# Turned-row copies, query statistics, late rows and first expert rows in another order (attention, router and experts on one core)

## The reference, cut to what matters

```python
# x (4, 1024, 256), ctx (4, 154, 256); 16 heads of 16; 8 experts of width 192, top 2; one shared expert
q = layernorm_heads(layernorm(x) @ Wq.T) * SCALE     # in heads of 16
k = layernorm_heads(ctx @ Wk.T); v = ctx @ Wv.T
x = x + (softmax(q @ k.T) @ v) @ Wp.T + bp
h = layernorm(x)
scores = sigmoid(h @ W_gate_router)
sel = top_k(scores + expert_bias, 2); w = scores[sel] / sum(scores[sel])
shared = (silu(h @ Wg_s) * (h @ Wu_s)) @ Wd_s
routed = sum over the two e in sel of w_e * (silu(h @ Wg[e]) * (h @ Wu[e])) @ Wd[e]
return x + shared + routed
```

## Time and profile before

| | |
|---|---|
| median of three runs | 539.19 us |
| profiled execution, its own time | 539.25 us |
| its span | 537.4 us |
| mean granted TensorE clock | 0.971 |
| PE, DVE, ACT, POOL busy | 476.9, 314.9, 300.8, 213.2 us |
| attention loop | to about 253 us |
| shared stage | to about 332 us |
| experts | from 337 us |

### The profile page before, as it was taken

The page is one execution under the profiler, slowest core; times in us unless marked ns, Lnnn a source line. Parts: engine busy times, 40 slices in busy tenths (PEclk is TensorE's granted clock), DMA queues, the critical chain, the costliest instruction groups (busy, mean ns, idle before and its releaser), DMA issues.

```text
span 537.4 us, 12057 instructions
## 1 busy us (share of the span) xinstructions
PE 476.9 (89%) x3324; PEld 313.0 (58%) x3325; DVE 314.9 (59%) x965; ACT 300.8 (56%) x544; POOL 213.2 (40%) x186
## 2 busy tenths in 40 slices
PE   4867899999899979888999995799999998999990
PEld 3743344444444435333554542799989987988980
DVE  3995466767877587555837872255555545445550
ACT  1577878888777785565333011455655654555540
POOL 4113211111011853045453253056655557555654
PEclk9999999999999998899999999699999999999996
DMA  7959301111101311033347554545766756575654
GB/s 232 339 187 355 155 20 40 41 41 56 39 26 39 121 67 54 20 119 127 119 139 233 162 189 138 148 79 98 122 97 94 125 85 100 99 118 88 102 79 46
DMA packets 43703, 60.99 MB, mean 113 GB/s; under 512 B 6512, under 2 KB 34672, under 8 KB 42992
## 3 DMA queue, kind: packets, MB, share of 16 engines
q1 hardware_dynamic: 28768, 37.45, 23.0%
q0 software_dynamic: 14896, 23.08, 21.5%
HBM read 34.29 MB, written 29.39 MB: 118 GB/s over the span
## 4 chain that ended last, share of the span: by engine, by line
PE 47%; DVE 12%; issue 11%; DMA 11%; ACT 11%; POOL 2%; SPq 2%; POOLq 2%; DVEq 0%; ACTq 0%
PE bankS L1114 7%; PE bankS L1105 7%; ACT attn L642 6%; DMA out<-VR,attn 6%; PE bankV L939 5%; PE bankR L795 4%; PE bankS L1033 4%; PE bankQ L1105 3%; PE bankR L1105 3%; DMA sorted_rows<-XR,route 3%; PE bankV L943 2%; POOL sorted_rows L496 2%; PE bankQ L795 2%; DVE OTT L1337 1%; DVE rec L1335 1%
## 5 line engine op out<-in xcount | busy, mean ns | idle before, releaser
L553 POOL DMA_INDIRECT out<-VR,attn x71 | 109.6, 1544 | 91.1 <-DVE VR L1573 40.7
L496 POOL DMA_INDIRECT sorted_rows<-XR,route x64 | 63.5, 993 | 86.3 <-PE bankD L945 22.8
L642 ACT ACTIVATE attn<-bankS,bias 128x512 f32<-128x512 f32 x128 | 81.0, 680 | 11.9 <-PE bankS L911 11.6
L755 ACT ACTIVATE attn<-experts 128x768 f32 x72 | 60.5, 843 | 24.0 <-issue 23.9
L939 PE MATMUL bankV<-attn,VS 128*32 128x512 f32 x256 | 62.8, 613 | 3.7 <-DVE OTT L1337 3.5
L941 PE MATMUL bankD<-attn,ON 128*32 128x512 f32 x256 | 62.8, 613 | 0.0
L1105 PE MATMUL bankS<-scores_in,attn 128*128 128x128 f32 x432 | 55.2, 287 | 2.8 <-issue 2.6
L1105 PEld LDWEIGHTS bankS<-scores_in,attn 128*128 128x128 f32 x432 | 52.1, 199 | 9.0 <-issue 9.0
L472 POOL DMA_DIRECT2D x_in<-in_xT x13 | 9.5, 735 | 113.0 <-PE bankQ L795 112.0
L1573 DVE TENSOR_TENSOR VR<-bankS,attn 128x256 f32<-128x256 f32 x71 | 30.2, 425 | 27.3 <-PE bankS L1114 14.0
L1114 PE MATMUL bankS<-experts,scores_in 128*128 x142 | 42.7, 383 | 0.4 <-DVE VR L1573 0.3
(11 more groups left out here) (272 smaller groups left out, 951.9 us busy)
## 6 DMA issues: line engine op xcount, KB each, us to landing
VS<-sorted_rows SPq DMA_DIRECT2D x72, 130.0 KB
x_cols<-X2T SPq DMA_DIRECT2D x16, 256.0 KB
out<-X SPq DMA_DIRECT2D x8, 512.0 KB
x_in<-in_xT POOLq DMA_DIRECT2D x15, 256.0 KB, 3.6
scores_in<-x_cols SPq DMA_DIRECT2D x14, 256.0 KB
experts<-in_wgu SPq DMA_DIRECT2D x2, 1536.0 KB, 9.7
X<-in_x SPq DMA_DIRECT2D x1, 2048.0 KB, 18.4
experts<-in_wd SPq DMA_DIRECT2D x2, 1024.0 KB, 14.8
```

What stands on the lines that cost most here:

```text
L496: pool.indirect_dma_start(sorted_rows.rearrange("s p r -> (s p) r"), bass.IndirectOffsetOnAxis(ap=index, axis=0), rows, None, bounds_check ...
L553: pool.indirect_dma_start(out, bass.IndirectOffsetOnAxis(ap=dest[:, i:i + 1], axis=0), y_out[:, i % 4], None, bounds_check=B * N + SPARE - ...
L642: act.activation(Pb[:, u % 2, c, :], bankS[:, c % GH, :], ACT.Exp, bias=bias[:, b, GH * g + c:GH * g + c + 1] if c < GH else biasR[:, b, g ...
L755: act.activation(w_cur[:, k], wgu_sb[:, :, ds(e_, 1), :].rearrange("p c o f -> p c (o f)"), ACT.Copy).then_inc(f_w["e"], 1)
```

## The change

- ScalarE, even units from 26 on: `out_columns(m)` stands ahead of `denominators(u - 2)` and the fifth exponential, not behind them.
- VectorE, units 16 and 24 (where the first selection of a part, `scored` and `best(0)`, stands in the odd unit just before): `stats` stands behind `norm`, ahead of `spreads`.
- Shared stage, TensorE: the late rows are turned ahead of the first two parts of step 2; the logits go ahead of `shared_down(1)`; `counts` of the last part go from step 4 to step 3, there behind `shared_down(2)`. ScalarE: the exponential of the last logits stands between the two gates of step 2. VectorE: the last part's selection, sums and places move ahead of shared products.
- Experts: the second half of the first group's rows is turned behind `up(1)` and copied behind the first gate.

```diff
--- before.py
+++ after.py
@@ -688,10 +688,12 @@
                         if m >= 0:
                             out_root(m)
                         exps(u, (2, 3))
+                        if pc >= PIECES:
+                            out_columns(m)
                         if u >= 2:
                             denominators(u - 2)
                         exps(u, (4,))
-                        if m >= 0:
+                        if m >= 0 and pc < PIECES:
                             out_columns(m)
                         c, step = divmod(m, PP)
                         if c >= 1 and step == 0:
@@ -741,13 +743,10 @@
                 act.activation(late_r[:, k], late_mv[:, k, :, 1], ACT.Ln, bias=eps[:, :]).then_inc(l_ln, 1)
                 act.wait_ge(l_ln, k + 1)
                 act.activation(late_r[:, k], late_r[:, k], ACT.Exp, scale=-0.5).then_inc(l_or, 1)
-            def columns(a):
-
-
-                for h in range(2):
-                    act.wait_ge(f_xt["e"], 2 * a + (h + 1))
-                    act.activation(x_col[:, 2 * h:2 * h + 2], row_bank(h).rearrange("p (t c) -> p t c", t=2), ACT.Copy) \
-                        .then_inc(f_xc["e"], 1)
+            def columns(a, h):
+
+                act.wait_ge(f_xt["e"], 2 * a + (h + 1))
+                act.activation(x_col[:, 2 * h:2 * h + 2], row_bank(h).rearrange("p (t c) -> p t c", t=2), ACT.Copy).then_inc(f_xc["e"], 1)
 
             def weights(a, k):
 
@@ -763,8 +762,11 @@
                         act.activation(act_g[:, k], gate_bank(k)[:, 0:2 * P], ACT.Silu).then_inc(f_si[kind], 1)
                         if more(a, tiles) and k < of_four(a + 1, tiles):
                             weights(a + 1, k)
+                        if isinstance(a, int) and a == 0 and k == 0:
+                            columns(0, 1)
                     if more(a, tiles):
-                        columns(a + 1)
+                        for h in range(2):
+                            columns(a + 1, h)
                 return gates
 
             shared_second(1)
@@ -772,15 +774,16 @@
                 act.wait_ge(l_xt, k + 1)
                 act.wait_ge(x2t_st[k], 16 * (LATE // 2))
                 act.activation(X2T[:, k, :], late_bank[k], ACT.Copy).then_inc(l_xs, 1)
-            shared(2)
+            shared_first(2)
             logit_exps(PARTS - 1)
+            shared_second(2)
             for a in range(3, QUADS):
                 shared(a)
             act.wait_ge(w_in, 16 * (KC + FC))
             act.wait_ge(routed, 1)
             weights(0, 0)
             weights(0, 1)
-            columns(0)
+            columns(0, 0)
             weights(0, 2)
             weights(0, 3)
             quads(act, SLOTS, ffn("e", SLOTS))
@@ -1065,17 +1068,17 @@
             shared_up(1, 1)
             shared_down(0)
             shared_up(1, 2)
-            shared_up(2, 0)
-            shared_up(2, 1)
             for k, m in enumerate(late):
                 pe.wait_ge(l_x2, k + 1)
                 turn_two(late_bank[k], XR[:, TT * m:TT * m + TT]).then_inc(l_xt, 1)
-            shared_down(1)
+            shared_up(2, 0)
+            shared_up(2, 1)
             pe.wait_ge(l_xs, 2)
             logits(late_bank[0]).then_inc(l_lg, 1)
-            shared_up(2, 2)
+            shared_down(1)
             pe.wait_ge(l_done, 1)
             logit_rows(late_bank[1])
+            shared_up(2, 2)
 
             def expert(tile):
                 return pe.value_load(etile[0:1, ds(tile, 1)], min_val=0, max_val=E - 1)
@@ -1118,6 +1121,8 @@
                     e_ = [expert(4 * a)] + [None] * 3
                     for k in range(tiles_):
                         up(k, e_[k])
+                        if isinstance(a, int) and a == 0 and k == 1:
+                            transposes(0, 1)
                         if k < tiles_ - 1:
                             e_[k + 1] = expert(4 * a + (k + 1))
                         if k >= 2:
@@ -1134,9 +1139,9 @@
 
                 shared_up(a, 0)
                 shared_up(a, 1)
-                if a == PARTS:
+                shared_down(a - 1)
+                if a == 3:
                     counts(PARTS - 1, late_bank[0])
-                shared_down(a - 1)
                 shared_up(a, 2)
 
             for a in range(3, QUADS):
@@ -1146,7 +1151,6 @@
             pe.wait_ge(routed, 1)
             pe.wait_ge(h_zero, 1)
             transposes(0, 0)
-            transposes(0, 1)
             quads(pe, SLOTS, ffn("e", SLOTS))
 
         @block.vector
@@ -1436,13 +1440,16 @@
                     u, pc = G * n + g, q_piece(n, g)
                     if g % 2 == 0:
                         m = 2 * n - 3 + g // 2
-                        if pc < PIECES:
+                        behind_best = u // 2 >= 8 and (u // 2 - 8) % PP == 0
+                        if pc < PIECES and not behind_best:
                             stats(TT * pc, TT)
                         if m >= 0:
                             out_rows(m)
                         if u >= 2:
                             norm(u - 2)
                         if pc < PIECES:
+                            if behind_best:
+                                stats(TT * pc, TT)
                             spreads(pc, 0)
                         if m >= 0 and m % 2 == 1:
                             out_logits(m)
@@ -1635,20 +1642,20 @@
             dve.wait_ge(l_lg, 1)
             dve.tensor_copy(LGT[:, 1, :], late_bank[0][:, 0:P]).then_inc(l_done, 1)
             shared_result(1)
-            shared_second(2)
             scored(PARTS - 1)
             best(0)
             taken(0)
-            shared_first(3)
+            shared_second(2)
             best(1)
             taken(1)
             counted(PARTS - 1)
+            shared_first(3)
             weights(PARTS - 1)
             shared_result(2)
+            sums_of(PARTS - 1, late_bank[0])
+            places_of(PARTS - 1)
             shared_second(3)
             shared_first(4)
-            sums_of(PARTS - 1, late_bank[0])
-            places_of(PARTS - 1)
             spare_rows()
             shared_result(3)
             shared_second(4)
```

## The result

| | before | after |
|---|---|---|
| median of 13 runs each | 537.67 us | 545.67 us |
| lowest and highest | 535.27, 543.64 | 541.64, 549.37 |
| profiled execution | 539.25 | 542.38 |
| its span, mean granted clock | 537.4, 0.971 | 540.6, 0.965 |

The ratio is 1.016, with a 95% interval of 1.0135 to 1.0186. The sign was forecast, the size was not: 541.6 with a range to 544.5. The two profiles are 3.2 us apart in span, the medians 8.0. By the ratio it is 8.6 us. The ratio is not the quotient of the two medians; it leaves out runs more than 1.5% above the fastest of their kernel, as before's 543.64 is.

A forecast was written before the change was run, and what follows sets the result against it. TensorE, busy 89%, bounds the kernel, so edits count only at its idle places or clock falls. 539.25 + 3.8 + 1.7 - 1.6 + 0 - 0.3 - 1.2 = 541.65, said as 541.6 us, range 537.0 to 544.5.

The forecast's parts named there:

- What bounds the kernel: TensorE busy 89% of the span; late even units chain from ScalarE's reciprocal over VectorE's normalisation to `weighted`.
- The sum: All terms added to the profiled 539.25 us give 541.65, said as 541.6.
- Part 1: Units 26, 28, 30: ScalarE's copy ahead of the denominators delays the logarithm by 1.1, 1.3 and 1.4 us; +3.8.
- The clock: Units 28 and 30: one further fall of TensorE's clock from added idleness, +1.7 us, bounds 0 and 3.4.
- Part 2: Statistics behind the normalisation: unit 24 gains 1.6 us (ends -1.1 and -2.8), unit 16 comes to 0.
- Part 3: Shared stage, late rows, counts and places moved up: gain and loss nearly cancel, -0.3 us (ends -3.0 and +2.0).
- Part 4: Ahead of the experts, half of the first rows turned behind two gate products: -1.2 us (ends -0.3 and -2.0).
- rival D: Earlier stores lengthen the second and third scatter groups, +2.0 instead of -0.3: 543.9 us; chance 0.12.
- A: Rival: TensorE's clock never falls further in the late even units, 539.9 us; chance 0.22.
- B: Rival: scatters follow the earlier places, nearly filling the gap ahead of the experts, -4.9 instead of -0.3: 537.0; chance 0.13.
- C: Rival: ScalarE's copy move costs nothing, its delay hidden and no clock fall: 536.1 us; chance 0.06.

The follow-up runs named there:

- fill_after: Changed kernel with matmuls that nobody reads in the three idle places of units 26, 28 and 30; 538.09 us, ratio to before 1.0025.
- fill_undo: Changed kernel with ScalarE's copy back behind the fifth exponential and seven unread matmuls ahead of logits or counts in units 26, 28, 30; 534.81 us, ratio 0.9951.
- copy_between: Kernel before with ScalarE's copy between the denominators and the fifth exponential in units 26, 28 and 30; 537.81 us, ratio 0.9998.
- only_late: Kernel before with only the late rows, counts and places moved up; 538.11 us, ratio 1.0028.
- only_rows: Kernel before with only the second half of the first rows turned behind two gate products; 537.52 us, ratio 1.0005.
- best_nolate: fill_undo with six unread fp32 matmuls ahead of the experts, and late rows, counts and places where before has them; 531.95 us, ratio to before 0.9923.
- undo_copy: Changed kernel with only ScalarE's copy put back behind the fifth exponential; 536.24 us, ratio to before 0.998.
- only_copy: Kernel before with only ScalarE's copy moved ahead of the denominators in the late even units; 545.03 us, ratio 1.017.

## Why the prediction was wrong, point by point

**What bounds the kernel** held. In the late even units the way from the reciprocal over the normalisation to `weighted` is the chain; `fill_after` against `fill_undo` measures its delay with the clock whole in both.

**The sum.** The forecast was 2.4 us above before (541.65 against 539.25), the ratio says 8.6, so 6.2 were missing. The copy cost 9.7 instead of 5.5: 0.2 of that difference is waiting, 4.0 the clock. The rest of the change gave 1.1 (up to 2.3) instead of 3.1: 2.0.

**Part 1, the waiting: +3.8 forecast, 4.0 measured.** The three pieces of idleness came out as 0.69, 1.1 to 1.3 and 1.0 to 1.1 against the forecast 0.65, 1.2 and 1.05, and the reciprocal at 6.08 us against 6.1.

**The clock: +1.7 forecast, about 5.7 measured (3.8 to 7.6; 4.2 between the two profiles). This is the step that failed,** and in two ways. First, I counted one fall between bounds of none and two, each a half of 3.4 us, for units 28 and 30. After's profile shows a stretch twice as long at unit 28 (6.8 us, which cost 2.7) and one at unit 30 (1.5). My upper bound of 3.4 for the term was no bound: it took from before the length of one stretch and assumed that a unit can't have two. The rule of the Trainium skill that I set beside it (TensorE: Matmul & The Clock Gate, there under "A second HAM failure mode: psum-queue depth-cycling", not in the part on thin-M) pointed to the larger figure, and the windows of after agree with it, at 0.50; in `copy_between` pauses of 1.03 and 0.59 passed at full clock. Second, I took before's profiled execution as the level and read from it which idleness makes the clock fall. It held two falls, of which I wrote that unit 26 had its own already; `only_late` and `only_rows`, other executions of the same loop, had none and one, after the same 2.44 and 1.78 us. A time that hangs on falls of the clock needs more than one trace of before.

**Part 2: -1.6 forecast, -0.8 (-2.0 to +0.4) measured.** The steps are as told: unit 24's idleness is 1.18, unit 16's gain at the rows is given back at the turned queries. At unit 16 GpSimd's addition no longer met VectorE's second instruction (0.19 us in after), as I had left open; the Trainium skill's rule on the shared port pair (SBUF — State Buffer) is neither contradicted nor tested by that. What I may have priced too high is the fall at unit 24: it was in before's profile and not in `only_late`'s, so it isn't always there to be saved. The interval holds the -1.6 too.

**Part 3: -0.3 forecast, +1.5 (0.1 to 2.8) for the part alone.** The places came earlier and released nothing. GpSimd's scatters in after, first the second group's landing beside the earlier stores, then the last part's first scatter, released by a landing and no longer by VectorE's place as in the earlier trace rows, then the last group:

```profile
287.69 0.97 POOL L496 DMA_INDIRECT sorted_rows<-XR,route  x1 [4.31 <-DMA sorted_rows<-XR,route]
...
306.34 0.97 POOL L496 DMA_INDIRECT sorted_rows<-XR,route  x1 [4.11 <-DMA sorted_rows<-XR,route]
...
332.58 0.97 POOL L496 DMA_INDIRECT sorted_rows<-XR,route  x1 [2.95 <-DMA sorted_rows<-XR,route]
```

The second group's wait became 4.31 (2.47 in before), as rival D and the rule of the Trainium skill (DMA: Bandwidth & Descriptors, Queues, rings and completion order) have it. But stores aren't needed for a long landing: in `best_nolate` the first group's took 4.55, with nothing issued by SyncE between 255.7 and 274.4 and the DMAs silent from 269.00 to 271.00. That the earlier stores made the 4.31 is likely, not shown. A row of GpSimd's timeline and one of the windows, of `best_nolate`:

```profile
270.61 0.97 POOL L496 DMA_INDIRECT sorted_rows<-XR,route  x1 [4.55 <-DMA sorted_rows<-XR,route]
...
269.00:271.00 2.00, 2.00 (x6) 0.81 (x5) 0.39 (x1) 0.59 (x1) 0.39 (x1) 1.00 0.00 0
```

The last part's first scatter came 46.7 us behind the loop's end, in before 45.3, so 1.4 later, where I had said less than 2 us earlier. But the last group started 73.0 behind it against 73.1: the later groups caught up, and D's price isn't there.

**Part 4: -1.2 forecast, +0.3 (-0.9 to +1.4) measured.** TensorE in after ahead of the experts: first half turned, two gate products, second half, third tile.

```profile
343.31 1.09 PE L1092 MATMUL bankV<-id,VS 128*128 128x128 f32 x4 [4.41 <-DMA VS<-sorted_rows]
345.08 4.85 PE L1108 MATMUL bankS<-scores_in,attn 128*128 128x128 f32 x24 [0.69 <-ACT scores_in L749]
349.77 0.60 PE L1092 MATMUL bankD<-id,VS 128*128 128x128 f32 x4
351.05 1.60 PE L1108 MATMUL bankQ<-scores_in,attn 128*128 128x128 f32 x12 [0.69 <-ACT scores_in L749]
```

From the first turning to the third tile it is 7.74 instead of 9.11, the new wait for ScalarE's copy is 0.69 (forecast 0.7 to 1.2). Of these 1.4 us, 0.5 are the two gate products (4.85 against the earlier trace rows's 5.35), which ran partly at full clock; the new order gives 0.9. The step is right, though smaller; that it reaches the end isn't shown.

The middles of parts 2 to 4 alone add up to +1.0, where `undo_copy`, all three together, has -1.1. Each is uncertain by 1.2 to 1.4, so this is no contradiction, and no evidence for any one of them.

**The rivals.** A (no further fall) is refuted by every trace with the copy ahead and no fillers. B and C are out, C by `only_copy`, B by `only_late`.

## What to carry to other kernels

An instruction that must wait itself may be moved ahead of another only if what stands behind it isn't on the chain; here a copy of 0.5 us with a wait of 0.7 went ahead of the reciprocal that releases TensorE, to shorten a wait on TensorE that had two others right behind it. Where TensorE has idle places like those behind which its clock has been seen to fall, price not only the wait but what a lower clock does to the full stretch behind it: here it cost about as much as the wait or more (4 to 6 against 4.0). It can be tested in one run, by filling the idle place with matmuls that nobody reads, and that filler may itself be worth keeping: with fillers in both places the kernel was 0.8 to 0.9% faster than before.

## What the runs showed of the hardware

- The same loop had no, one or two low stretches of the clock in different executions, after the same idleness (2.44 and 1.78 us), each about 3.4 us long and worth 1.6 to 1.7. That is some 3 us of the scatter between runs of before (535.3 to 541.1, and one at 543.6); one trace doesn't tell a kernel's typical number of falls.
- A low stretch can go on while TensorE is full: at unit 28 of after it lasted from 233.1 to 239.9, with no idleness from 234.35 on.
- GpSimd's wait for four scatters to land took from 2.3 to 6.3 us. It was 4.55 in one place where the DMAs were silent from 269.00 to 271.00 (`best_nolate`).
- Idleness of 2.9 us in three pieces lowered the clock in each of the three units of after. In `copy_between` 1.20 and 0.59 of it did so at unit 26, while 1.03 and 0.59 at unit 28 and 0.97 and 0.59 at unit 30 didn't.
- An fp32 matmul is two instructions in the records: 384 columns, twelve matmuls, x24, 8.0 us, about 0.33 us each instruction at full clock.
